# First attention: tokens turned by VectorE and two transfers, squares summed by a multiply, query bias seeded in PSUM

## The reference

```
h = x * rsqrt(mean(x * x) + 1e-6) * norm1_w          # over the channels
h = h * (1 + scale[:, None, :]) + shift[:, None, :]  # scale, shift = cond @ film1_w + film1_b
Q, K, V = h @ q_w + q_b, h @ k_w + k_b, h @ v_w + v_b
attn = softmax(Q @ K^T * D ** -0.5)
x = x + (attn @ V) @ proj_w + proj_b
```

## Time and profile before

| what | us |
|---|---|
| median of 3 runs (1572.06 to 1572.91) | 1572.86 |
| the profiled execution | 1573.35 |
| its span in the trace | 1571.5 |
| TensorE busy in the span | 1538.2 (98%) |
| VectorE, ScalarE, GpSimd busy | 1294.1, 874.9, 387.4 |

### The profile page before, as it was taken

One profiled execution on the slowest core, in us unless ns is written; L12 is line 12 of the kernel. 1 busy time (PEld: TensorE's weight loads), 2 busy tenths in 40 slices (PEclk: granted clock), 3 DMA queues, 4 the chain that ended last, 5 costly groups with the idle time before them and its releaser, 6 DMA issues.

```text
span 1571.5 us, 42382 instructions
## 1 busy us (share of the span) xinstructions
PE 1538.2 (98%) x14314; PEld 1381.8 (88%) x14314; DVE 1294.1 (82%) x2953; ACT 874.9 (56%) x1753; POOL 387.4 (25%) x525
## 2 busy tenths in 40 slices
PE   8999999999999999999999999999997999999999
PEld 7999998999999998677777777777775999999999
DVE  5798888787777787888888888888885888888886
ACT  3566664344444453667777767777765344444443
POOL 2333332010000013243443343443333200000000
PEclk9999999999999999999999999999999999999999
DMA  6700002211111112333333333333331233232232
GB/s 174 223 21 20 20 20 63 77 43 48 47 52 41 53 48 66 109 102 99 109 107 103 108 108 97 107 107 101 107 111 55 83 101 100 94 95 93 100 100 68
DMA packets 147505, 132.84 MB, mean 85 GB/s; under 512 B 23568, under 2 KB 130128, under 8 KB 147424
## 3 DMA queue, kind: packets, MB, share of 16 engines
q1 hardware_dynamic: 147264, 131.74, 26.5%
q0 software_dynamic: 160, 0.04, 0.1%
HBM read 54.75 MB, written 24.54 MB: 50 GB/s over the span
## 4 chain that ended last, share of the span: by engine, by line
PE 91%; DVE 5%; issue 2%; DMA 1%; ACT 1%; DVEq 0%; SPq 0%; POOL 0%; POOLq 0%; ACTq 0%
PE bank L216 63%; PE bank L1788 8%; PE bank L1770 7%; PE bank L1732 5%; PE bank L1798 2%; PE bank L400 2%; PE bank L1806 1%; PE bank L778 1%; PE bank L473 1%; PE bank L198 1%; PE bank L564 0%; DMA A_w_film<-in_L_cond_film_w 0%; DVE C_negmax L1744 0%; DVE m_xhat L1744 0%; DVE m_h_lo L313 0%
## 5 line engine op out<-in xcount | busy, mean ns | idle before, releaser
L1879 ACT ACTIVATE C_probs<-bank 128x1024 f32<-128x1024 f32 x256 | 263.4, 1029 | 156.2 <-PE bank L1770 153.7
L1744 DVE TENSOR_REDUCE C_negmax<-bank 128x4 f32<-128x1024 f32 x248 | 303.4, 1223 | 46.5 <-PE bank L1732 43.0
L1114 ACT ACTIVATE D_g<-bank,D_bias 128x256 f32<-128x256 f32 x256 | 107.5, 472 | 197.7 <-PE bank L216 197.7
L1114 ACT ACTIVATE B_g<-bank,B_bias 128x256 f32<-128x256 f32 x256 | 107.6, 472 | 196.8 <-PE bank L216 196.6
L365 POOL TENSOR_TENSOR m_small<-m_small,consts 128x2 f32<-128x2 f32 x64 | 47.8, 747 | 590.5 <-DVE m_small L359 306.1
L216 PE MATMUL bank<-B_wt_w_hi,B_g_lo 128*128 128x256 f32 x512 | 143.0, 279 | 3.5 <-DVE B_g_lo L1124 3.4
L1770 PEld LDWEIGHTS bank<-C_qs,C_kx 64*128 64x128 f32 x1024 | 77.5, 185 | 78.3 <-ACT C_probs L1879 46.1
L216 PE MATMUL bank<-D_wt_w_hi,D_g_lo 128*128 128x256 f32 x512 | 141.7, 277 | 1.5 <-DVE D_g_lo L1124 1.5
L216 PE MATMUL bank<-m_h_hi,D_wt_w_lo 128*128 128x256 f32 x512 | 141.7, 277 | 0.8 <-DVE m_h_lo L419 0.8
L216 PE MATMUL bank<-m_h_hi,B_wt_w_lo 128*128 128x256 f32 x512 | 141.7, 277 | 0.0
L216 PE MATMUL bank<-B_wt_w_hi,B_g_hi 128*128 128x256 f32 x512 | 141.5, 276 | 0.0
(11 more groups left out here) (267 smaller groups left out, 4835.8 us busy)
## 6 DMA issues: line engine op xcount, KB each, us to landing
C_qs<-C_q_hi SPq DMA_DIRECT2D x128, 128.0 KB
C_kx<-C_k_hi SPq DMA_DIRECT2D x128, 128.0 KB, 2.6
C_qs<-C_q_lo SPq DMA_DIRECT2D x64, 128.0 KB
C_kx<-C_k_lo SPq DMA_DIRECT2D x64, 128.0 KB, 2.1
C_gbc<-mod_rows SPq DMA_DIRECT2D x32, 256.0 KB, 3.4
D_gbc<-mod_rows SPq DMA_DIRECT2D x32, 256.0 KB, 3.4
turned<-N_blocks SPq DMA_DIRECT2D x31, 256.0 KB, 2.0
N_back<-turned SPq DMA_DIRECT2D x124, 64.0 KB, 2.0
```

Source lines behind the costliest of these rows:

```text
L1114: ins = eng.activation(o, p, func, bias=per_seq(bias1, 2 * u + d, b))
L1744: e_max.by(eng.tensor_reduce(m4[:, :, :, j], spair[:, :].rearrange("p (e q k) -> p e q k", e=2, q=TH), AX, ALU.max, negate=True))
L1879: e_exp.by(eng.activation(probs[t % NP][:, :], stpair[:, :], ACT.Exp, scale=scl))
```

## The change

In phase A, from the third sequence on (the first two stay as they are):

- T goes from TensorE. VectorE turns a_xhat into A_blocks, SP stores that in DRAM (turn out), and fetches it (turn back) into A_back; hi_h and lo_h read A_back.
- The fetch is one transfer of 256 KB in the place of four, in phases B and D too. For that the order of tokens changes: token n of half h is now at 2n + h. The turn reads its source with a step of 4 elements and writes with a step of 2; S takes each second column of the query as its stationary operand; in B and D, GELU reads PSUM with a step of 2 and writes without one.
- Statistics: two SCALAR_TENSOR_TENSOR per sequence, x times 1/256 times x, each with its sum as a second output, then one addition of eps. The products themselves go into A_w_m, which nobody reads. (Phases B, C and D keep BN_STATS.) The statistics no longer wait for the last xhat.
- Query bias: ScalarE writes the bias into the bank ahead of q (seed), which then accumulates on it. There are two banks for it, taken in turn. hi_q and lo_q become one instruction each.
- New places in the tables. On ScalarE xhat of sequence i now stands ahead of hi_h of i-1.

```diff
-                self.e_back = event("turn_back", 16 * QUADS, first)
+                self.e_back = event("turn_back", 16, first)
...
-                    self.blocks.rearrange("p (c t h i) -> p h t c i", c=QUADS, h=TH, t=KT),
-                    n.xhat[:, :].rearrange("p (h t c i) -> p h t c i", c=QUADS, h=TH, t=KT)))
+                    self.blocks.rearrange("p (c t i h) -> p h t c i", c=QUADS, h=TH, t=KT),
+                    n.xhat[:, :].rearrange("p (h t i c) -> p h t c i", c=QUADS, h=TH, t=KT)))
...
-                for c in range(QUADS):
-                    self.e_back.by(eng.dma_start(
-                        self.back[BLOCK * c:BLOCK * (c + 1), :].rearrange("p (a x) -> p a x", a=QUADS),
-                        turn_dram[:, c * P:(c + 1) * P].rearrange("(a i) x -> i a x", a=QUADS)), 16)
+                self.e_back.by(eng.dma_start(
+                    self.back.rearrange("p (a x) -> p a x", a=QUADS),
+                    turn_dram.rearrange("(a i) (c x) -> (i c) a x", a=QUADS, c=QUADS)), 16)
...
+                if self.squares is not None:
+                    self.e_rstd.wait(eng, b.back(1))
+                    for h in range(TH):
+                        ins = eng.scalar_tensor_tensor(out=self.squares[:, h * D:(h + 1) * D], in0=x_at(b)[:, h],
+                                                       scalar=1.0 / D, in1=x_at(b)[:, h], op0=ALU.mult, op1=ALU.mult,
+                                                       accum_out=self.mv[:, h:h + 1])
+                    self.e_mv.by(ins)
+                    self.e_mv.wait(eng, b)
+                    self.e_var.by(eng.tensor_scalar(self.var[:, :], self.mv[:, 0:TH], EPS, None, ALU.add))
+                    return
...
-                T_ACT = {"xhat": 9.5, "hi_h": 23.5, "hi_q": 33.5, "hi_v": 37, "exp": 45, "hi_p": 54.5}
-                T_DVE = {"stats": 0.5, "lo_h": 25.5, "lo_q": 35.5, "lo_v": 38, "max": 43.5, "lo_p": 55, "res": 62}
+                T_ACT = {"xhat": 6.9, "hi_h": 24.5, "hi_q": 33.5, "hi_v": 37, "exp": 45, "hi_p": 54.5, "seed": 26.5}
+                T_DVE = {"stats": 0.5, "lo_h": 26.3, "turn": 10.5, "lo_q": 35.5, "lo_v": 38, "max": 43.5, "lo_p": 55, "res": 62}
...
+                    def seed(b):
+                        if not bias_first(b):
+                            return
+                        e_lo["q"].wait(eng, b.back(UNROLL))
+                        bias = biasq[:, :].rearrange("p (t j u) -> p t j u", t=KT, u=UNROLL)[:, :, b.pair, b.par:b.par + 1]
+                        e_seed.by(eng.activation(bQ[b.par][:, :].rearrange("p (t n) -> p t n", t=KT),
+                                                 bias.broadcast_to([P, KT, S]), ACT.Copy))
...
-                            o = o.rearrange("p (h a i) -> p a h i", h=TH, a=QUADS)
-                            p = p.rearrange("p (a h i) -> p a h i", h=TH, a=QUADS)
+                            o = o.rearrange("p (h n) -> p h n", h=TH)
+                            p = p.rearrange("p (n h) -> p h n", h=TH)
```

More of the change, by code:

```diff
@@ L319, in build, with __init__ @@
         class Norm:
-            def __init__(self, buffers, event, rms, scale, bank, reader, centred=False):
+            def __init__(self, buffers, event, rms, scale, bank, reader, centred=False, squares=None):
                 self.rms, self.scale, self.bank, self.reader = rms, scale, bank, reader
@@ L328, in __init__ @@
                 n = buffers.name
+                self.squares = squares
                 self.e_mv = event(n + "mv")
-                self.e_msq = event("msq") if rms else None
+                self.e_msq = event("msq") if rms and squares is None else None
                 self.e_var = event(n + "var")
@@ L741, in q_proj @@
                         norm.e_lo.wait(eng, b)
-                        e_lo["q"].wait(eng, b.back(1))
+                        if bias_first(b):
+                            e_seed.wait(eng, b)
+                        else:
+                            e_lo["q"].wait(eng, b.back(1))
                         for t in range(KT):
                             c = [slice(k * D + t * P, k * D + (t + 1) * P) for k in range(KT)]
-                            ins = mm3(eng, bQ[:, t * S:(t + 1) * S],
-                                      [((m_hi[:, c[k]], m_lo[:, c[k]]), norm.tokens(b, k)) for k in range(KT)])
+                            ins = mm3(eng, bQ[b.par][:, t * S:(t + 1) * S],
+                                      [((m_hi[:, c[k]], m_lo[:, c[k]]), norm.tokens(b, k)) for k in range(KT)],
+                                      start=t == 0 and not bias_first(b), skip=True)
                         e_q.by(ins)
@@ L760, in transpose_x @@
                     def transpose_x(b):
+                        if turn.turns(b):
+                            return
                         norm.e_lo.wait(eng, b.back(1))
@@ L767, in scores @@
                         for qh in range(TH):
-                            c = [slice(t * S + qh * P, t * S + (qh + 1) * P) for t in range(KT)]
+                            if turn.turns(b):
+                                c = [slice(t * S + qh, (t + 1) * S, TH) for t in range(KT)]
+                            else:
+                                c = [slice(t * S + qh * P, t * S + (qh + 1) * P) for t in range(KT)]
                             ins = mm3(eng, bS[:, qh * S:(qh + 1) * S],
@@ L834, in scalar @@
                         "B hi": lambda b: heads["B"].norm.evac_hi(eng, b), "B gelu0": lambda b: heads["B"].gelu(eng, b, 0),
-                        "xhat": lambda b: norm.normalize(eng, b), "hi_h": lambda b: norm.evac_hi(eng, b),
-                        "hi_q": hi_q,
+                        "xhat": lambda b: norm.normalize(eng, b), "hi_h": lambda b: (turn if turn.turns(b) else norm).evac_hi(eng, b),
+                        "hi_q": hi_q, "seed": seed,
                         "hi_v": lambda b: hi_plain(b, "v", bV, v_hi[b.par], e_v, UNROLL), "exp": exp,
@@ L842, in low_q @@
                         e_hi["q"].wait(eng, b)
+                        if bias_first(b):
+                            e_lo["q"].by(eng.tensor_tensor(q_lo[:, :], bQ[b.par][:, :], q_hi[:, :].bitcast(F32), ALU.subtract))
+                            return
                         for t in range(KT):
                             c = slice(t * S, (t + 1) * S)
-                            ins = eng.scalar_tensor_tensor(out=q_lo[:, c], in0=bQ[:, c], scalar=per_seq(biasq, t, b),
+                            ins = eng.scalar_tensor_tensor(out=q_lo[:, c], in0=bQ[b.par][:, c], scalar=per_seq(biasq, t, b),
                                                            in1=q_hi[:, c].bitcast(F32), op0=ALU.add, op1=ALU.subtract)
@@ L882, in vector @@
                         "mlp bias": lambda b: mlp.add_biases(eng, pmod, 0),
-                        "stats": lambda b: norm.stats(eng, b, x_in), "lo_h": lambda b: norm.evac_lo(eng, b),
+                        "stats": lambda b: norm.stats(eng, b, x_in), "lo_h": lambda b: (turn if turn.turns(b) else norm).evac_lo(eng, b), "turn": lambda b: turn.turns(b) and turn.turn(eng, b),
                         "lo_q": low_q,
@@ L942, in sync @@
                         "B turn1": b_turn,
-                        "row": load_row, "film2": load_film2, "ada": load_ada, "late loads": late_loads} | {
+                        "turn out": lambda b: turn.turns(b) and turn.send(eng, b),
+                        "turn back": lambda b: turn.turns(b) and turn.fetch(eng, b), "row": load_row, "film2": load_film2, "ada": load_ada, "late loads": late_loads} | {
                             f"x{c}": lambda b, c=c: load_x(eng, X_FIRST + c * X_CHUNK, X_CHUNK, x_in[3][0])
```

18 lines of the change are left out of this document (14 added, 4 removed).

## The result

| | before | after |
|---|---|---|
| median of the runs | 1572.91 us (5 runs, 1572.06 to 1574.90) | 1656.77 us (5 runs, 1654.58 to 1662.02) |
| ratio of the medians, 95% interval | 1 | 1.0535 (1.0519 to 1.0552) |
| profiled execution, span | 1573.35, 1571.5 us | 1660.50, 1658.7 us |

The change makes the kernel 84 us slower. The prediction had the direction (1588.5, range 1576 to 1613) and the mechanism, but a fifth of the size.

A forecast was written before the change was run, and what follows sets the result against it. It took TensorE to bound the steady iterations before (6.50 us), and a ring of waits through the transfers after (6.92). Steady +9.7, load iterations +6.9 and MLP start -1.0 sum to +15.6 us: 1588.5 us, range 1576 to 1613.

The forecast's parts named there:

- the ring: First attention: turn, store, fetch, high half, low half, next turn hold one iteration, so none is shorter than 6.92 us.
- its five parts: Turn to store 0.75, store to fetch 2.04, fetch 2.4, high to low half 0.94, low half to next turn 0.79 us.
- the high half waiting for A_back: Sign in the changed profile: ScalarE's high half waits for the fetch; if it never does, the forecast is wrong.
- low to turn: VectorE's low half of the previous sequence to the start of the next turn, taken as the usual 0.79 us.
- The rows of 6: Earlier trace's first turn of the MLP behind the first attention; its low pair, meeting a GpSimd instruction, took 1.55 us.
- my +9.7: Steady part of the first attention: 0.42 us more in each of 23 iterations, +9.7 us.
- the load iterations: Six first-attention iterations while inputs and weights load: stores land late behind loads, 59.0 us instead of 52.1, +6.9 us.
- The second ring: First attention: low half, turn, maximum, reciprocal, residual, statistics, root, normalising, high half; 6.8 us (6.6 to 7.0).
- the slow stride: Rival on VectorE's turn: 16-byte steps double the time per element, 0.54 us more in both rings; 1604 us, chance 0.04.
- The statistics: VectorE's accumulating multiplies and small add taken at 1.25 us; rival at half throughput: 0.54 us more, 1599 us, chance 0.09.
- The start of the first MLP: ScalarE waits there for the turn; a fetch of 2.4 instead of 3.35 us brings that forward, -1 us.
- Heavy: Rival: the first attention's fetch takes 3.4 us, as the gates' read does; ring 7.92, total 1619 us, chance 0.14.

The follow-up runs named there:

- the row-early run: The changed kernel with SP issuing the projection row ahead of the next store instead of behind the fetch; 1630.01 us, ratio 1.0364 to the kernel before.
- the loads ahead: The changed kernel with SP issuing film2's and ada's weights ahead of sequence 2's store and the MLP's behind sequence 3's fetch; 1643.81 us, ratio 1.0448.

## Why the prediction was wrong

**The bound and the mechanism were right.** It named the ring, its five parts, the order on VectorE that makes it, and the view to look at first (the high half waiting for A_back). The run with the turn moved ahead confirms it, with 34 us of the 65 that I expected of it, since another loop closed at 7.3.

**The sum of the ring was wrong: 6.92 for 8.74.** Part by part: turn to store 0.75, measured 1.11; store to fetch 2.04, measured 2.03; fetch 2.4, measured 2.80 (inside the bounds of 2.0 and 3.4); high to low 0.94, measured 1.07; low to turn 0.79, measured 1.73. Half of the miss is in the last term, and it is the step that failed: "The rows of 6 show 1.55 us for a pair that meets a GpSimd instruction; I take the usual one." The row was on the table and I took the other without following who starts GpSimd's addition. The store and the fetch stand ahead of the row on SP, and so tie that addition to the low pair in most iterations. By my own sum this term alone, 0.94 us in 23 and 6 iterations, is 27 us and gives 1616, past the end of my range; the row-early run, which takes it out, is 27 us faster, though only 17 of that in the steady part. The whole miss of the ring, 1.82 us in 22 iterations, is 40 us; the steady part is 38 over my +9.7.

**Where the rest is.** The span grew by 71.6 us more than the forecast: 38.3 in the steady part, 19.9 in the load iterations, 12.5 ahead of the first reciprocal, 1 at the start of the MLP.

**The second ring was close.** I had it at 6.8 us and missed it by the same low pair and the longer turn. ScalarE's high half waits only 0.45 us for the fetch in the turn shown, and the normalising in front of it begins right behind the root. So that ring stands at some 8.3 of the 8.74, and a faster fetch alone could not have given more than about 0.45 us an iteration.

**The turn's stride.** I had the turn at 0.71 us by the copies of the earlier trace rows and gave the slow stride 0.04. The groups of VectorE, after:

```profile
L278 DVE STREAM_TRANSPOSE N_blocks<-m_xhat 128x512 f32<-128x512 f32 x31 | 34.1, 1100 | 3.0
```

It is 1.10 us here and 1.08 in the attention, 0.37 to 0.40 more, in all three phases. The Trainium skill ("SBUF — State Buffer", The DMA port swizzle) says that each access into a new 16-byte line costs; by that rule the trace agrees here. The turn writes with a step of 2 as well, and no run separates the two. The step that misled me was a comparison with a copy of 128 elements: by my own line through the turns, 174 of its 308 ns do not depend on the length (an estimate). 0.37 is less than my 0.54, the rival's time of 1604 missed as well, and behind the first attention, where it is longer too, the span did not grow.

**The statistics were right to doubt, wrong in size.** I took 1.25 us, and they take 0.88 to the next start. VectorE's groups in the run without the turn:

```profile
L346 DVE DVE_READ_ACCUMULATOR A_w_m<-xres 128x1 f32 x64 | 5.2, 81 | 0.0
```

The multiplies are 0.41 us each and the readout 81 ns, most of it hidden. The Trainium skill ("Vector Engine (DVE) Microarchitecture Reference", Points that are easy to get wrong) has this form at half throughput with two sources in SBUF that are not bf16; the trace disagrees: 0.41 us for 256 elements, less than the 0.44 of one that reads PSUM.

**The load iterations: right effect, wrong size.** Stores behind a chunk landed 5.5, 6.4 and 6.7 us after their issue, 3.5 to 4.7 late, as said (3.4). The first of them:

```profile
91.37 0.33 SPq L284 DMA_DIRECT2D turned<-A_blocks  x1
96.88 0.38 SPq L288 DMA_DIRECT2D A_back<-turned  x1
```

But the six took 78.9 us where I had 59.0. The ring is 1.82 longer here too, 11 us in six. And I did not go down SP's queue for the other entries: the weights of film2, ada and the MLP stand behind fetches that wait, and 12.0 us come back in these iterations with the loads ahead (the two overlap; their sum is over the 19.9). I had put the start at nothing without looking; it lost 12.5 us, 6.0 of them in the wait for film2, 3.3 before any turn. With the loads ahead only 1.7 of the 12.5 come back.

**The start of the first MLP** (-1): nothing. The fetch is 0.5 us shorter and the turn 0.4 longer. GELU's stride of two in PSUM costs nothing, as counted: 471 ns for 472.

**The rivals.** "Heavy" (1619) came nearest, 38 us short, with a ring of 7.92 for 8.74 and for the wrong reason: it had the fetch at 3.4 us, which measured 2.80. The range ended at 1613 because the bounds of the pieces were taken one at a time. All at their ends (1.29 to the store with the slow stride, 2.04, 3.4, 0.94, 1.55 for the low half) give 9.2 us and a time above 1640.

## What to carry to other kernels

Before work is moved from an engine to a transfer, write down the order of every queue that it passes and look for the ring: what stands behind the waiting instruction, and whether the instruction that starts the next transfer is there. Here it is 7.0 us from a turn to its low half, more than an iteration of 6.5. With only one sequence on that way the change cost 84 us, and two changed slots, with the waits that let two be on it, took 56 of that back. Go down the issuing queue as well (the small row, the weights), since what stands behind a wait moves with it; and when a trace shows two durations for one instruction, find out which one applies rather than taking the usual.

## What I had not expected of the hardware

- After the change, a pair of 256-wide three-operand instructions on VectorE takes 1.35 to 1.81 us where GpSimd's addition of two tensors starts within 0.45 us of it, and 0.88 where it starts 0.54 us behind or later. GpSimd's addition mostly takes 1.60 us then, and 1.45 when alone.
- One fetch of 256 KB takes 2.80 us to the first reader, four of 64 KB take 3.35 to 3.48, of which SP needs 1.75 to issue them.
- Moving operands in runs of 32 columns cost TensorE nothing that shows: 6.29 us an iteration with them and without.
- Two 256-wide multiplies on GpSimd (1.19 us) come close to ScalarE's 0.91.
